# A four-block transformer kernel: scores ahead of the value fold, a bf16 bias product, an earlier opening of the last attention, and Silu on ScalarE in the last mixture

## The chip, the cores and the metric

The kernel runs on one NeuronCore of one Trainium2 chip. The metric is the device time of one execution in microseconds (us); several executions are given, and their median is the time compared. The profile is of one execution of its own.

## The reference

The input x has 4 blocks of 512 tokens of 256 numbers in float32. Four attentions and four feed-forward layers follow each other; each adds a gated term to x.

```python
x = x + tanh(g_xattn[0]) * L0_xattn(layernorm(x), ctx, mask)   # 16 heads, 64 keys, softmax per head
x = x + tanh(g_ffn[0])   * L0_ffn(layernorm(x))                # quantised gated FFN, 704 wide
x = x + tanh(g_xattn[1]) * L1_xattn(layernorm(x), ctx)         # one head
x = x + tanh(g_ffn[1])   * L1_ffn(layernorm(x))                # mixture: 8 experts, top 2, relu squared
x = x + tanh(g_xattn[2]) * L2_xattn(layernorm(x), ctx)         # one head
x = x + tanh(g_ffn[2])   * L2_ffn(layernorm(x))                # top 1, one shared weight, with bias b_expert
x = x + tanh(g_xattn[3]) * L3_xattn(layernorm(x), ctx)         # 16 heads, scores clipped to +-11
x = x + tanh(g_ffn[3])   * L3_ffn(layernorm(x))                # mixture: 8 experts, top 2, silu; shared expert
# L3_ffn: h = silu(x @ w1[e]);  y = h @ w2[e];  routed = sum of topw * y
# L2_ffn: expert_out = dispatched @ w_expert + b_expert
```

## The kernel before

The eight layers are stages 0 to 7 of one program. All five queues (SP, POOL, PE, ACT, DVE) are written out by hand, in the order of the code; an instruction waits for counts of semaphores. x stays in SBUF, and a block is four tiles of 128 tokens. Each pipe has two PSUM buffers, used in turn: `pt` for transposes, `sh` for scores and hidden values, `ob` for outputs. `product` (line 701) is nearly every matmul, `transposes` (line 669) every transposition, `move` (line 1277) ACT's copy out of `pt`.

Stage 0 begins with `fold16`. The context's keys and values are multiplied into the weights once, so that the scores of a tile are one product of 128 tokens with 1024 columns (16 heads times 64 keys), and the output one product with `valsO`. On PE that is: keys and values of the context, transposes of Wq, eight products for the folded keys (line 735), eight for the folded values (line 745). ACT moves the first half of each and DVE the second (lines 1328 to 1330 and 1746 to 1762); between them DVE has the other work of the `between` table, LayerNorm statistics and the row maxima of the quantised weights (`row_max`), after which POOL may round these weights (`to_int`, waits for `q_inv`).

`attend16(stage)` is the attention with 16 heads, in stages 0 and 6. PE does for every tile t: transposes of the probabilities of t (they wait for `prob_ready`), scores of tile t+2, output product of t. In stage 0 DVE adds the mask (L1788), takes the maximum of each head (L1791), subtracts it (L1793), waits for ACT's one Exp over 1024 columns (L1340), sums the heads (L1801), and multiplies by the reciprocals (L1805). The probabilities have two buffers. In stage 6 the scores are clipped (L1796) instead of shifted. After each block DVE takes the statistics of the new x (L1657), in stage 0 its extremes too (L1778).

Stage 5 does per block: router logits, two output products of two tiles each with the bias as a third factor (`ones[0:1]` times `be2[0:1]`, in float32), and between them the folding of stage 6's keys and values (`fold_units`, counted by `f_full` and `f_taken`).

Stage 6 opens with `fold_done`: DVE adds the bias bo3 to the folded values (L2395) after stage 5's last statistics, and PE's first scores wait for it. SP then loads w1 of the last mixture into `raw1`; POOL splits it into `wB`, four times a copy (L635) and a subtraction (L583).

The mixtures (stages 3 and 7) send the rows to DRAM by expert, fetch pairs of 128 rows back and run `NPAIR` = 20 pairs through a pipeline: transposes, product with w1 (`expert_up`), activation, transposes, product with w2 (`expert_back`). In stage 7 the activation of a pair is ACT's Tanh (L1507) and then DVE's (1 + t) * u (L2167); the missing 0.5 is in the weights wK (`weigh`).

## Time and profile before

| | us |
|---|---|
| median of 3 executions | 954.27 |
| lowest, highest | 948.47, 955.95 |
| the profiled execution, its own time | 944.84 |
| its span | 943.1 |
| PE busy in the span | 787.4 |
| DVE busy | 630.2 |
| ACT busy | 334.4 |
| POOL busy | 283.0 |

The span is the time from the first to the last instruction, 1.7 us less than the execution's own time. A busy PE is not PE at its peak. In the views a row is a start and a duration in us, the engine, the line of the program, the operation, output and inputs by their names without buffer numbers, and in brackets the idle time before it and what ended it. Stage 0's attention runs from about 63 to 214, stage 5 from about 559 to 617, stage 6 from there to about 775, and stage 7's pairs from about 832 to 910.

### The profile page before, as it was taken

What the parts mean: (1) busy time and instruction counts of PE and PEld (TensorE: products, weight loads), DVE (VectorE), ACT (ScalarE), POOL (GpSimd) and SP (SyncE); (2) the same over time, 40 slices, a digit from 0 to 9 for tenths busy, and PEclk for the clock granted to TensorE, in tenths of its full rate; (3) what the DMA queues carried; (4) which work ended last, traced back from release to release, by engine and by line L of the source; (5) the groups of instructions that cost most, each with busy time, mean ns of one, the idle gap of its engine ahead of it and who ended that gap; (6) DMA issues with size and microseconds to landing.
All of it is one profiled execution on the core that took longest, in us unless ns stands there. A gap on an engine that the chain in (4) does not pass through costs nothing.

```text
span 943.1 us, 13461 instructions
## 1 busy us (share of the span) xinstructions
PE 787.4 (83%) x4214; PEld 593.6 (63%) x4216; DVE 630.2 (67%) x1698; ACT 334.4 (35%) x622; POOL 283.0 (30%) x284
## 2 busy tenths in 40 slices
PE   7688988965788777589989799978999998779992
PEld 6455656653256656379978676635676675479971
DVE  3678889866997666555637775556757655566646
ACT  2422231225644662134544543312233221235530
POOL 1038113160001556614561111234001234205540
PEclk9998999997999999779999998889999998889995
DMA  8629950000001002247426000051000011224427
GB/s 284 123 92 385 313 187 0 1 1 1 0 1 34 1 0 86 95 122 248 137 80 223 1 1 1 1 179 34 1 1 12 35 45 47 89 58 143 134 85 255
DMA packets 55474, 83.30 MB, mean 88 GB/s; under 512 B 14688, under 2 KB 44384, under 8 KB 55136
## 3 DMA queue, kind: packets, MB, share of 16 engines
q1 hardware_dynamic: 48496, 63.52, 21.8%
q0 software_dynamic: 6912, 18.95, 5.6%
q8 instruction: 36, 0.59, 0.3%
q14 instruction: 30, 0.25, 0.1%
HBM read 61.41 MB, written 37.95 MB: 105 GB/s over the span
## 4 chain that ended last, share of the span: by engine, by line
PE 50%; DVE 24%; ACT 8%; DVEq 6%; issue 6%; DMA 3%; POOL 2%; SPq 0%; ACTq 0%; POOLq 0%
PE sh L701 12%; PE ob L701 12%; PE sh L1077 6%; PE ob L1077 6%; PE pt L669 4%; DVE sm L1801 2%; DVE x L2043 2%; DVE work L1805 2%; DVE work L1793 2%; DVE mx L1791 2%; ACT work L1340 2%; PE pt L701 2%; DVEq L1790 2%; DVE stats L1657 2%; PE pt L1069 2%
## 5 line engine op out<-in xcount | busy, mean ns | idle before, releaser
L701 PE MATMUL sh<-area,xnT 128*128 128x512 f32 (+1 forms) x384 | 138.2, 509 | 7.0 <-issue 4.5
L701 PE MATMUL ob<-area,work 128*128 128x256 f32 x512 | 116.3, 380 | 9.0 <-ACT work L1277 9.0
L534 POOL TENSOR_TENSOR rstd<-var,minush 128x4 f32<-128x4 f32 (+1 forms) x29 | 30.4, 1047 | 303.6 <-DVE var L1664 303.6
L701 PEld LDWEIGHTS ob<-area,work 128*128 128x128 f32 x512 | 96.7, 190 | 34.6 <-issue 22.8
L598 POOL DMA_INDIRECT yt<-xn,work x80 | 76.7, 959 | 122.5 <-ACT xn L1521 106.9
L701 PEld LDWEIGHTS sh<-area,xnT 128*128 128x128 f32 x384 | 64.3, 199 | 59.6 <-issue 56.4
L1340 ACT ACTIVATE work<-work 128x1024 f32<-128x1024 f32 x32 | 33.8, 1058 | 174.5 <-DVE work L1793 93.6
L589 POOL DMA_INDIRECT xg<-area,dest x64 | 63.9, 999 | 70.4 <-DVE dest L2035 53.0
L669 PE MATMUL pt<-ident,work 128*128 128x128 f32 (+1 forms) x292 | 41.9, 284 | 24.7 <-DVE work L1805 10.8
L701 PE MATMUL ob<-area 128*128 128x256 f32 (+1 forms) x152 | 45.2, 458 | 15.8 <-DVE area L2061 9.0
L669 PEld LDWEIGHTS pt<-ident,work 128*128 128x128 f32 (+1 forms) x292 | 33.8, 142 | 32.8 <-issue 14.4
L701 PEld LDWEIGHTS ob<-area 128*128 128x128 f32 (+1 forms) x152 | 32.8, 220 | 28.4 <-DVE area L2061 10.8
L1801 DVE TENSOR_REDUCE sm<-work 128x16 f32<-128x1024 f32 x32 | 38.9, 1216 | 16.3 <-ACT work L1340 16.3
L1277 ACT COPY work<-pt 128x512 f32<-128x512 f32 (+1 forms) x76 | 41.3, 582 | 16.2 <-PE pt L669 15.8
L1657 DVE BATCH_NORM_STATS2 stats<-x 128x6 f32<-128x256 f32 x128 | 45.0, 414 | 2.9
L1805 DVE TENSOR_TENSOR work<-work,rsm 128x1024 f32<-128x1024 f32 x32 | 41.0, 1282 | 2.4
L2157 DVE TENSOR_TENSOR xnTR<-pt,xnTR 128x512 fp32r<-128x512 f32 x40 | 27.6, 691 | 21.9 <-ACT xnTR L1501 21.9
L1077 PE MATMUL sh<-wB,xnTR 128*128 x240 | 35.7, 301 | 5.7 <-DVE xnTR L2157 5.7
L1507 ACT ACTIVATE work<-sh 128x512 f32<-128x512 f32 x40 | 23.9, 598 | 41.7 <-PE sh L1077 41.7
L701 PE MATMUL sh<-area 128*128 (+3 forms) x118 | 35.6, 446 | 2.9 <-DVE area L2307 2.6
L1521 ACT COPY xn<-ob 128x512 f32<-128x512 f32 x40 | 23.5, 587 | 39.8 <-PE ob L1077 29.7
L1712 DVE TENSOR_TENSOR x<-ob,x 128x256 f32<-128x256 f32 x32 | 13.4, 420 | 36.0 <-PE ob L701 36.0
(298 smaller groups left out, 1664.2 us busy)
## 6 DMA issues: line engine op xcount, KB each, us to landing
work<-xg SPq DMA_DIRECT2D x80, 129.0 KB, 2.3
area<-in_L_ffn_w SPq DMA_DIRECT2D x4, 2048.0 KB, 12.6
area<-yt SPq DMA_DIRECT2D x8, 1024.0 KB, 9.0
area<-in_L_xattn_Wq SPq DMA_DIRECT2D x2, 1024.0 KB, 9.7
x<-in_x SPq DMA_DIRECT2D x1, 2048.0 KB, 15.3
area<-in_L_xattn_Wo SPq DMA_DIRECT2D x2, 1024.0 KB, 16.0
area<-in_L_xattn_Wkv SPq DMA_DIRECT2D x2, 1024.0 KB, 6.3
out<-x SPq DMA_DIRECT2D x4, 512.0 KB, 2.9
```

The costliest lines, as they stand in the source:

```text
L534: pool.tensor_tensor(rstd[:, n], var[:, n], minush[:, n], ALU.pow).then_inc(given, 1)
L589: pool.indirect_dma_start(xg_rows[:, :], bass.IndirectOffsetOnAxis(ap=dest[:, b % 2, 2 * j + w:2 * j + w + 1], axis=0), xn_rows(stage, b)[ ...
L598: pool.indirect_dma_start(yt[:, :], bass.IndirectOffsetOnAxis(ap=back_to[:, 2 * i + q:2 * i + q + 1], axis=0), ypair[i % 2][:, q * D:(q + ...
L669: mm = pe.transpose(dst[0:r, c0:c1], src, (idn or ident)[0:src.shape[0], 0:src.shape[0]])
L701: mm = pe.matmul(o, a, b, start=(k == 0), stop=(k == len(lhs) - 1))
L1077: mm = pe.matmul(o, lhs[:, a, k * P:(k + 1) * P], w[:, b, bass.ds(off + k * D, D)], start=(k == 0 and t == 0), stop=(k == 1 and t == 2))
L1277: act.copy(dst, src[0:r, 0:cols_]).then_inc(pt_moved, 1)
L1340: act.activation(prob[i % 2], prob[i % 2], ACT.Exp).then_inc(exped[stage], 1)
L1657: dve.bn_stats(stats[:, j, :], tile(j) if tile else xt(b, j))
L1801: dve.tensor_reduce(sm[:, i % 2, :], heads(p), AX.X, ALU.add)
L1805: dve.tensor_tensor(heads(p), heads(p), over_keys(rsm[:, i % 2, :]), ALU.mult).then_inc(prob_ready[stage], 1)
L2157: dve.tensor_tensor(xnTR[:, 0, 1, (i % 2) * 512:(i % 2 + 1) * 512], pt[i % 2][:, :], xnTR[:, 0, 0, (i % 2) * 512:(i % 2 + 1) * 512].bitcas ...
```

## The change

1. Stage 0: the scores of tiles 0 and 1 stand between the folded keys and the folded values on PE. In ACT, the Exp of these tiles stands between the moves of the values; in DVE, `shift0` of both stands ahead of the values.
2. Stage 0: the maximum is no longer subtracted by DVE. It is negated and goes in as the bias of Exp, so Exp is one instruction for each head (16 of 64 columns for a tile), and each gives the head's sum by `accum_out`. DVE's mask and maximum are done in two halves of 8 heads, the first as soon as half of the scores is there (`scored_half`). The row maxima of the weights move from the fold into the first three tiles.
3. Stage 5: the bias is split into three bf16 parts in rows 0, 32 and 64 of `be2_parts` (over bo0's memory), by nine operations of DVE after a memset, ahead of the pairs of stage 3; the bias product is one of 96 rows of bf16 ones.
4. Stage 6: PE's first scores wait for `f_taken` and no longer for `fold_done`, which moves ahead of stage 5's blocks on DVE; w1 is loaded as soon as 8 units are folded, and its first part is copied by ACT (`raw_hi`) ahead of the first Exp. POOL keeps the subtractions.
5. Stage 7: the activation of a pair is ACT's Silu; DVE's instruction is gone, and the 0.5 leaves the weights.

```diff
+        SCORES0, VALUES0, FOLDED0 = start_of("sh", 0) + 12, start_of("sh", 0) + 14, start_of("sh", 0) + 22
@@ PE, fold16
+                first_norm_T(6, 1)
+                pe.wait_ge(pt_moved, 8)
+                pe.wait_ge(sh_taken, SCORES0)
+                scores16(0, 0, 0)
+                scores16(0, 0, 1)
+                n = VALUES0
@@ PE, attend16
                 if stage == 6:
+                    pe.wait_ge(sh_taken, start_of("sh", 6) + PRE["sh"][6])
+                    pe.wait_ge(f_taken, NFOLD)
+                    pe.wait_ge(pt_moved, start_of("pt", 6))
+                    scores16(6, 0, 0)
+                    scores16(6, 0, 1)
                     pe.wait_ge(fold_done, 1)
-                    pe.wait_ge(pt_moved, start_of("pt", 6))
+                else:
+                    pe.wait_ge(sh_taken, FOLDED0)
@@ PE, stage 5
-                                     [T(5, b)[:, k, j * P:(j + 1) * P] for k in range(KD)] + [ones[0:1, :]],
-                                     [wexp[:, k * D:(k + 1) * D] for k in range(KD)] + [be2[0:1, :]])
+                                     [T(5, b)[:, k, j * P:(j + 1) * P] for k in range(KD)] + [onesb[0:96, :]],
+                                     [wexp[:, k * D:(k + 1) * D] for k in range(KD)] + [be2_parts[0:96, :]])
@@ ACT
+            def exps0(i, first, last):
+                act.wait_ge(shifted[0], 2 * i + (2 if last > H // 2 else 1))
+                for h in range(first, last):
+                    p = prob[i % 2][:, h * C:(h + 1) * C]
+                    a = act.activation(p, p, ACT.Exp, bias=mx[:, i % 2, h:h + 1], accum_out=sm[:, i % 2, h:h + 1])
+                if last == H:
+                    a.then_inc(exped[0], 1)
+            def attend0():
+                for b in straight:
+                    for j in range(TB):
+                        i = b.u * TB + j
+                        for half in range(2):
+                            n = prob_fill(0, i, half)
+                            move(n, n % 2, probT[:, half * 512:(half + 1) * 512])
+                        if i + 2 < NT:
+                            exps0(i + 2, 0, H // 2)
+                        if j == 1 and b.u + 1 < NB:
+                            norm_move(0, b, 4)
+                        if i + 2 < NT:
+                            exps0(i + 2, H // 2, H)
+                act.wait_ge(in_w6, 16)
+                for b in range(NB):
+                    q = slice(b * 1024, (b + 1) * 1024)
+                    act.copy(wB[:, 0, q], raw1[:, q]).then_inc(raw_hi, 1)
+                            act.activation(hpair[m % 2], u, ACT.Silu).then_inc(h_ready[7], 1)
@@ DVE
+            def shift0(i):
+                n, slot = score_fill(0, i // TB, i % TB)
+                for c in range(2):
+                    q = slice(c * 512, (c + 1) * 512)
+                    p = prob[i % 2][:, q]
+                    dve.wait_ge(*((scored_half, i + 1) if c == 0 else (sh_full, n + 1)))
+                    ins = dve.scalar_tensor_tensor(heads(p), mask[:, i, :].unsqueeze(1).broadcast_to([P, H // 2, C]), -FMAX,
+                                                   heads(sh[slot][:, q]), ALU.mult, ALU.add)
+                    if c == 1:
+                        ins.then_inc(sh_taken, 1)
+                    dve.drain()
+                    dve.tensor_reduce(mx[:, i % 2, c * H // 2:(c + 1) * H // 2], heads(p), AX.X, ALU.max,
+                                      negate=True).then_inc(shifted[0], 1)
+            def normalise0(i):
+                p = prob[i % 2]
+                dve.wait_ge(exped[0], i + 1)
+                dve.reciprocal(rsm[:, i % 2, :], sm[:, i % 2, :])
+                dve.drain()
+                dve.tensor_tensor(heads(p), heads(p), over_keys(rsm[:, i % 2, :]), ALU.mult).then_inc(prob_ready[0], 1)
+            def attend0():
...
+                        if i >= 1:
+                            add(Block((i - 1) // TB), 0, (i - 1) % TB, [(i - 1) % TB])
+                        if i + 2 < NT:
+                            shift0(i + 2)
+                        if i + 1 < NT:
+                            normalise0(i + 1)
+                        if i < 3:
+                            row_max(i)
+                        if i == 3:
+                            weight_scales()
@@ POOL
-            pool.wait_ge(in_w7, 32)
             for b in range(NB):
                 q = slice(b * 1024, (b + 1) * 1024)
-                pool.tensor_copy(wB[:, 0, q], raw1[:, q])
-                pool.drain()
+                pool.wait_ge(raw_hi, b + 1)
                 rest(wB[:, 1, q], raw1[:, q], wB[:, 0, q], raw_split)
@@ SP
-            sp.wait_ge(f_taken, NFOLD)
+            sp.wait_ge(f_taken, 8)
+            load(raw1.rearrange("p (e n) -> p e n", e=2 * NE), rows(I["L3_ffn_w1"].rearrange("e d f -> (e d) f")), in_w6)
             sp.wait_ge(o_added, start_of("o", 6))
-            load(raw1.rearrange("p (e n) -> p e n", e=2 * NE), rows(I["L3_ffn_w1"].rearrange("e d f -> (e d) f")), in_w7)
             load(raw2.rearrange("p (e n) -> p e n", e=2 * NE), rows(I["L3_ffn_w2"].rearrange("e f d -> (e f) d")), in_w7)
```

Where the instructions stand. On PE, at the end of stage 0's fold (`area2` holds the context's values and Wo, `area1` the folded keys, `xnT` the normalised tokens, `work` the probabilities), before:

```order
L745 MATMUL sh0<-area2 128x256 [waits sh_taken]
L745 MATMUL sh0<-area2 128x256 x3
L745 MATMUL sh1<-area2 128x256 [waits sh_taken]
L745 MATMUL sh1<-area2 128x256 x3
L669 MATMUL pt0<-ident,xn 128x128 [waits pt_moved,ln_done]
L669 MATMUL pt0<-ident,xn 128x128 x3
L669 MATMUL pt1<-ident,xn 128x128 [waits pt_moved]
L669 MATMUL pt1<-ident,xn 128x128 x3
L701 MATMUL sh0<-area1,xnT 128x512 [waits sh_taken,pt_moved]
L701 MATMUL sh0<-area1,xnT 128x512 x3
L701 MATMUL sh1<-area1,xnT 128x512 [waits sh_taken]
L701 MATMUL sh1<-area1,xnT 128x512 x3
```

and now, where the last products of the folded keys (line 757) are followed by them:

```order
L757 MATMUL sh1<-work 128x256 [waits sh_taken]
L757 MATMUL sh1<-work 128x256 x3
L679 MATMUL pt0<-ident,xn 128x128 [waits pt_moved,ln_done]
L679 MATMUL pt0<-ident,xn 128x128 x3
L679 MATMUL pt1<-ident,xn 128x128 [waits pt_moved]
L679 MATMUL pt1<-ident,xn 128x128 x3
L711 MATMUL sh0<-area1,xnT 128x512 [waits sh_taken,pt_moved]
L711 MATMUL sh0<-area1,xnT 128x512 x3
L711 MATMUL sh1<-area1,xnT 128x512 [waits sh_taken]
L711 MATMUL sh1<-area1,xnT 128x512 x3
L773 MATMUL sh0<-area2 128x256 [waits sh_taken,in_wo]
L773 MATMUL sh0<-area2 128x256 x3
```

The block's first transposes and the scores of two tiles have gone ahead of the eight value products; after these the transposes of the first probabilities follow at once.

On ACT, at the start of stage 0's attention (`sm` are the heads' sums, `mx` their maxima), before:

```order
L1330 ACTIVATE area1<-sh1,gates 128x512 [waits sh_full]
L1277 COPY xnT<-pt0 128x512 [waits pt_full]
L1277 COPY xnT<-pt1 128x512 [waits pt_full]
L1340 ACTIVATE work<-work 128x1024 [waits shifted0] x2
L1277 COPY work<-pt0 128x512 [waits pt_full]
L1277 COPY work<-pt1 128x512 [waits pt_full]
```

and now, from the last value move on:

```order
L1362 ACTIVATE area1<-sh1,gates 128x512 [waits sh_full]
L1298 COPY work<-pt0 128x512 [waits pt_full]
L1298 COPY work<-pt1 128x512 [waits pt_full]
L1321 ACTIVATE work,sm<-work,mx 128x64 [waits shifted0]
L1321 ACTIVATE work,sm<-work,mx 128x64 x7
L1321 ACTIVATE work,sm<-work,mx 128x64 [waits shifted0]
L1321 ACTIVATE work,sm<-work,mx 128x64 x7
```

One Exp of 1024 columns for a tile has become two groups of eight, and it now stands behind the moves of the tile two before it.

On PE, where stage 6 opens, before (`prob_ready6` is that tile 0's probabilities are there):

```order
L701 MATMUL ob1<-be2,ones 128x256
L701 MATMUL sh0<-area1,xnT 128x512 [waits pt_moved,sh_taken,fold_done]
L701 MATMUL sh0<-area1,xnT 128x512 x3
L701 MATMUL sh1<-area1,xnT 128x512 [waits sh_taken]
L701 MATMUL sh1<-area1,xnT 128x512 x3
L669 MATMUL pt1<-ident,work 128x128 [waits pt_moved,prob_ready6]
```

and now:

```order
L711 MATMUL ob1<-bo0,onesb 128x256
L711 MATMUL sh0<-area1,xnT 128x512 [waits pt_moved,sh_taken,f_taken]
L711 MATMUL sh0<-area1,xnT 128x512 x3
L711 MATMUL sh1<-area1,xnT 128x512 [waits sh_taken]
L711 MATMUL sh1<-area1,xnT 128x512 x3
L679 MATMUL pt1<-ident,work 128x128 [waits pt_moved,prob_ready6,fold_done]
```

The wait for `fold_done` has moved behind both scores.

## Rows read from the trace of the kernel before

**Rows 1.** TensorE in order of time, stage 0's attention.
```profile
74.28 1.97 PE L669 MATMUL pt<-ident,work 128*128 128x128 f32 x8 [4.46 <-DVE work L1805]
76.04 5.71 PE L701 MATMUL sh<-area,xnT 128*128 128x512 f32 x8
...
137.35 1.04 PE L669 MATMUL pt<-ident,work 128*128 128x128 f32 x8
138.22 3.60 PE L701 MATMUL sh<-area,xnT 128*128 128x512 f32 x8
...
145.11 1.04 PE L669 MATMUL pt<-ident,work 128*128 128x128 f32 x8
...
204.60 3.69 PE L701 MATMUL ob<-area,work 128*128 128x256 f32 x16 [3.14 <-ACT work L1277]
...
209.99 3.69 PE L701 MATMUL ob<-area,work 128*128 128x256 f32 x16 [0.82 <-ACT work L1277]
```

**Rows 2.** Busy time of each engine in one stretch of it.
```profile
73.90:200.40 126.50, 116.32 (x472) 79.14 (x473) 111.59 (x148) 31.45 (x48) 46.57 (x36) 0.97 0.47 156
```

**Rows 3.** VectorE in order of time, stage 0's attention.
```profile
97.72 1.23 DVE L1805 TENSOR_TENSOR work<-work,rsm 128x1024 f32<-128x1024 f32 x1
...
105.80 1.23 DVE L1805 TENSOR_TENSOR work<-work,rsm 128x1024 f32<-128x1024 f32 x1
...
113.28 2.34 DVE L1778 TENSOR_REDUCE xmm<-x 128x4 f32<-128x1024 f32 x2
```

**Rows 4.** ScalarE in order of time: a tile's two moves, and stage 2's Exp.
```profile
103.68 1.05 ACT L1277 COPY work<-pt 128x512 f32<-128x512 f32 x2
...
305.72 0.35 ACT L1417 ACTIVATE work<-work,mx 128x64 f32<-128x64 f32 x1 [1.81 <-DVE mx L1870]
306.07 0.33 ACT L1417 ACTIVATE work<-work,mx 128x64 f32<-128x64 f32 x1
```

**Rows 5.** All engines in order of time, stage 0's folded values.
```profile
56.12 2.00 PE L745 MATMUL sh<-area 128*128 128x256 f32 x8 [0.38 <-DVE area L1762]
57.51 0.74 DVE L1762 TENSOR_SCALAR area<-sh,gates 128x512 f32<-128x512 f32 x1
```

**Rows 6.** TensorE in order of time, one pair of products of stage 5.
```profile
585.15 0.69 PE L701 MATMUL ob<-be,ones 1*128 1x256 f32 x2
585.77 1.13 PE L701 MATMUL ob<-area,xnT 128*128 128x256 f32 x4
```

**Rows 7.** The chain that ended last, in order of time.
```profile
278.66 3.35 PE ob L1217 x24
...
616.88 4.46 issue
621.34 6.20 PE sh L701 x8
...
653.46 5.13 PE sh L701 x8
```

**Rows 8.** VectorE and TensorE in order of time, stages 5 and 6.
```profile
573.86 1.38 DVE L1670 TENSOR_SCALAR xn<-x,mv,rstd 128x256 f32<-128x256 f32 x4
...
619.97 1.27 DVE L2395 SCALAR_TENSOR_TENSOR area<-bo,gates,area 64x1024 f32<-64x1024 f32 x1
...
632.81 1.09 PE L669 MATMUL pt<-ident,work 128*128 128x128 f32 x8 [1.85 <-DVE work L1805]
...
642.79 2.21 DVE L1805 TENSOR_TENSOR work<-work,rsm 128x1024 f32<-128x1024 f32 x1
644.92 4.26 DVE L1670 TENSOR_SCALAR xn<-x,mv,rstd 128x256 f32<-128x256 f32 x4
```

**Rows 9.** GpSimd in order of time, the last subtraction of the split.
```profile
646.04 2.35 POOL L583 TENSOR_TENSOR wB<-area,wB 128x1024 fp32r<-128x1024 f32 x1
```

**Rows 10.** VectorE and TensorE: start of stage 3's and of stage 7's pairs.
```profile
405.67 0.69 DVE L2157 TENSOR_TENSOR xnTR<-pt,xnTR 128x512 fp32r<-128x512 f32 x1 [8.72 <-ACT xnTR L1501]
...
841.89 1.67 PE L1077 MATMUL ob<-wA,hidR 128*128 x12 [0.58 <-DVE hidR L2182]
```

More of the change, by code:

```diff
@@ L702, in product, with scores16 @@
                 return mm
+            def scores16(stage, u, j):
+                n, slot = score_fill(stage, u, j)
+                sh_slot(n)
+                for c in range(2):
+                    mm = product(sh[slot][:, c * 512:(c + 1) * 512],
+                                 [T(stage, Block(u))[:, k, j * P:(j + 1) * P] for k in range(KD)],
+                                 [keysA[:, (k * NB + u) * H * C + c * 512:(k * NB + u) * H * C + (c + 1) * 512]
+                                  for k in range(KD)])
+                    if stage == 0 and c == 0:
+                        mm.then_inc(scored_half, 1)
+                mm.then_inc(sh_full, 1)
             def fold16(stage, cT_, in_k, in_v, in_q, in_o, loads):
@@ L794, in attend16 @@
                         if j < 2:
-                            scores(b.u, j + 2)
+                            scores16(stage, b.u, j + 2)
                         elif b.u + 1 < NB:
@@ new lines, in normalise0 @@
+            def normalise0(i):
[5 more added lines that the diff above has]
+            def attend0():
+                for b in straight:
+                    for j in range(TB):
+                        i = b.u * TB + j
+                        pb = Block(b.u - 1)
+                        if i >= 1:
[8 more added lines that the diff above has]
+                            weight_scales()
+                        if b.u >= 1 and j == 0:
+                            norm_stats(pb)
+                        if b.u >= 1 and j == 1:
+                            extremes(pb)
+                        if i == 0:
+                            norm_next(0, straight[0], xn_free(0, straight[0], 5))
+                        if j == 3 and b.u + 2 < NB:
+                            norm_next(0, straight[b.u + 1], xn_free(0, straight[b.u + 1], 5))
+                add(straight[-1], 0, TB - 1, [TB - 1])
+                norm_stats(straight[-1])
+                extremes(straight[-1])
@@ L2035, in place, with bias_parts @@
                 dve.tensor_copy(dest[:, b.u % 2, :], destf[:, :, :].rearrange("p j w -> p (j w)")).then_inc(placed[stage], 1)
+            def bias_parts():
+                dve.memset(be2_parts[:, :], 0.0)
+                for r, before in ((0, 0), (32, 1), (64, 2)):
+                    row, part = be2[r:r + 1, :], be2_parts[r:r + 1, :]
+                    for _ in range(before):
+                        dve.drain()
+                        dve.tensor_copy(part, row)
+                        dve.drain()
+                        dve.tensor_tensor(row, row, part, ALU.subtract)
+                    dve.drain()
+                    ins = dve.tensor_copy(part, row)
+                ins.then_inc(bias_split, 1)
             def combine(stage, b):
@@ L2389, in route5 @@
                     ins.then_inc(o_added, 1)
+            v0 = valsO[0:64, 0:NB * D].rearrange("p (b d) -> p b d", b=NB)
+            dve.wait_ge(f_taken, 14)
+            dve.scalar_tensor_tensor(v0, bo3[0:64, :].unsqueeze(1).broadcast_to([64, NB, D]), gates[0:64, 3:4], v0,
+                                     ALU.mult, ALU.add).then_inc(fold_done, 1)
             for b in straight:
```

154 lines of the change are left out of this document (63 added, 91 removed).

## The prediction, made before the changed kernel ran

> **What bounds the kernel now.** I read the chain of waits first, by engine and then in order of time, and after it the timelines of the stages that the diff touches. PE carries half of the chain; DVE's part lies in stage 0 and at the openings. So each edit is worth what PE waits there, or what it takes away from PE's own stream.
>
> Stage 0's attention: in the middle of a block the transposes of successive tiles stand 7.76 us apart with no idle before them (137.35 to 145.11), the transposes taking 0.87 and the rest being scores and outputs [rows 1]. PE is the bound there, and DVE just keeps up: 8.1 us from one tile's normalising to the next (97.72 to 105.80 [rows 3]), for five passes over 1024 columns of about 1.23 and an Exp between them. Where DVE also has a block's extremes (2.34) and statistics, PE starves. From 73.90 to 200.40 PE is busy 116.32 of 126.50, so it stands idle for 10.2 [rows 2]. At the start it waits 4.46 for the first probabilities, and its first scores then take 5.71 instead of 3.60, since its clock has fallen to the lower level after that idle time [rows 1]. At the end it waits 3.14 for ACT, whose Exp and moves follow DVE [rows 1].
>
> Stage 5 is PE's own stream. The opening of stage 6 is a wait: PE ends stage 5 at 616.88, then nothing for 4.46 (`fold_done`, which DVE reaches at 619.97 behind the last statistics) [rows 7, 8], then two scores at the lower clock, the first 6.20 [rows 7], then 1.85 more until tile 0's probabilities at 632.81 [rows 8]. At tile 2 it waits again: a normalisation on DVE takes 2.21 and the four of xn 4.26, where the same four take 1.38 in stage 5, and the scores after that stall again run slowly, 5.13 [rows 7, 8].
>
> **The change part by part.** Sums are against the profiled execution's 944.84 us, of which 943.1 is the span.
>
> *Stage 0, loop.* For a tile DVE now has two half masks and two half maxima of 512 columns, each about 0.69 (such an operation of 512 columns takes 0.69 [rows 10]), and normalising 1.23 plus a small reciprocal [rows 3], with the add about 5 us against 7.76. ACT has 16 Exps at a pitch of 0.35 (305.72 to 306.07, with the accumulator's read inside it, the nearest row there is) and two moves of 1.05: 5.6 + 1.1 = 6.7 [rows 4]. Both fit under PE. So do the waits, counted from the end of a tile's scores, S. The first half was there 1.7 earlier, so its Exps run from S - 0.2 to S + 2.6, the second half's to S + 5.4, and the next moves to S + 6.5; the output product that needs them starts at S + 7.76. DVE ends the second half at S + 1.4 and the normalising of the next tile at S + 3.0; PE's transposes want it at S + 3.45. The margin is 0.45, the thinnest of the plan. A block's statistics or extremes (2.1 and 2.34) now lie in the time in which DVE waits for the next half score.
>
> PE's own work is then: 14 tiles of 7.76, 108.6; the last two without scores, 5.4 each (204.60 to 209.99 [rows 1]), 10.8; three transposes of a new block with their moves, about 1.4 each, 4.2. Together 123.6. Before, from 74.28 to 209.99 + 3.69 = 213.68, it was 139.4. Gain 15.8 at most. I take 14.5, leaving 1.3 for the first three tiles, where DVE has the row maxima (about 1.9 each) besides.
>
> *Stage 0, opening.* PE leaves the folded keys at about 41. The first block's transposes and their moves bring it to 43.4, two scores of 3.5 to 50.5. Eight value products of 2.00 [rows 5] would end at 66.5 if nothing waited. DVE holds them up: the first value's three operations (2.8), normalising tile 0 (1.6), and the statistics of two blocks (2.1 each) come between; by hand I get 69.2 for the last product and, with a move on ACT and DVE's 0.74 [rows 5], 70.6 for the start of the loop, against 74.28. ACT's Exps of both tiles (5.6 each) lie beside it. Gain 3.7. The bounds are 0 (the fold stretches by as much as it overlaps) and 5.
>
> *Stage 5.* The float32 bias takes 0.62 (585.15 to 585.77 [rows 6]), 16 times. A bf16 product of 128 by 256 takes 3.35 / 24 = 0.14 in stage 1 [rows 7]. 16 x 0.48 = 7.7; if changing from 128 rows to 96 and back costs as much again, 16 x 0.34 = 5.4. I take 7.5, since nothing else is late there: DVE idles for 6 us in a block. The split costs DVE a memset and nine operations of one row, 2 to 4 us, in a wait of 8.72 before stage 3's first pair [rows 10]: nothing; without that cover it would cost all of it. The earlier addition of bo3 (1.27 [rows 8]) delays stage 5's first block on DVE, whose one-hots are there some 2 us before PE asks.
>
> *Stage 6, opening.* Let E be the end of stage 5. The scores follow at once, at the full clock, to E + 6.9 (3.44 each, the pace of 138.22 in [rows 1]). DVE needs E + 3.4 for the last block's statistics, then clips at E + 3.6, and Exp, sum, reciprocal and product make E + 8.8 for PE's first transposes. Before it was 632.81 - 616.88 = 15.9. Gain 7.1. ACT's four copies (about 1 each) begin when its last small move is done, 3 before E, and end at E + 1, ahead of the first Exp at E + 4.9. They cost nothing unless w1 is late; it is loaded a hundred us earlier, behind the loads of stage 3's results. POOL's subtractions start behind its own last rstd, at E + 7.9, and take 4 x 2.35 [rows 9] to E + 17.4. The xn of the next block comes at E + 19.8, so it should take 1.38 and not 4.26, and the stall and slow scores after it go: 4.3 more by the same count of steps (its scores end 21.5 after the first transposes instead of 653.46 + 5.13 - 632.81 = 25.8 [rows 7, 8]). Gain 11.4.
>
> Those rows show DVE's operations between SBUF and SBUF stretched while POOL works, 4.26 for 1.38. The Trainium skill (GPSIMD Engine Reference, Key points) says that GpSimd shares its SBUF interfaces with VectorE and contends with instructions in a 2-port mode or with two SBUF inputs. By that rule the subtractions, which stay, still meet the normalising of tiles 0 and 1. The rival on this below is priced from rows.
>
> *Stage 7.* The pairs are PE's stream without gaps, so DVE's 0.69 less per pair is worth nothing there. Only at the start DVE's instruction stands ahead of one that PE waits 0.58 for [rows 10]. Gain 0.6; one more table load on ACT falls in a wait of 8 us for the first product. From -1.3 to 1.
>
> Sum: 14.5 + 3.7 + 7.5 + 11.4 + 0.6 = 37.7. That is 944.84 - 37.7 = 907 for an execution like the profiled one. The median before is 954.27, 9.4 above the profiled one, and the three range over 7.5. I put the same distance on the new kernel: 954.27 - 37.7 = 916.6. I say **916**.
>
> **The rivals.**
>
> *ACT becomes the bound in stage 0.* If the accumulator's read doesn't hide behind the next head's Exp and a head costs half as much again as in [rows 4], 0.54, a tile costs 16 x 0.54 + 1.05 = 9.7, and the loop's 14 tiles take 27 us more than PE's work: the loop loses about 12 on before instead of gaining 14.5. 37.7 - 26.5 = 11: **943**. Against it stands the pitch in [rows 4]. 6%.
>
> *The margin of 0.45 isn't there.* DVE's second half, drains and semaphores take a microsecond more than by my count, or POOL's rounding of the weights, which now runs beside the loop's tiles 4 to 14, stretches the normalising. Then PE waits about 0.6 a tile: 14 x 0.6 = 8.4, and **925**. For it: in [rows 8] such a product took 2.21. Against it: in tiles with POOL at work in stage 0 it took 1.23 [rows 3]. 17%.
>
> *The collision in stage 6 stays.* The subtractions run into the xn of the second block as before, because they start later or are themselves slowed: the 4.3 are lost, and 1 or 2 of the 7.1 with the normalising of tiles 0 and 1. **922**. This is where that rule of the Trainium skill leads. 15%.
>
> *The fold only stretches.* The scores' 7 us are added to the fold, since DVE and ACT paced it before, and the opening gives 0: **920**. 12%.
>
> *Slower.* The per-head Exps again, at a dearer price. The loop took 9.04 a tile before (126.50 / 14 [rows 2]); the rest of the change gives 23.2, or 1.66 a tile. So the whole is slower once ACT takes 10.7 a tile, that is 0.60 a head. At 0.65 (a wait for each accumulator before the next head) a tile is 11.5 and the total about 12 us slower than before, **966**. The row's 0.35 speaks against it; that the bias and sum here are columns of a 16-wide tile instead of 4 changes nothing that I can see. 2%.
>
> *It doesn't do what it says.* DVE's passes leave, but stage 0 isn't shorter, since PE's 7.76 bound it already. Only the idle 10.2, the slow start and the end can be won, and if all of these come from something else (the blocks' new xn, say), stage 0 gives 3: **932**. 3%.
>
> **How the numbers follow.** The forecast, 916, has 45%. With the next four rivals (925, 922, 920 and 932) lying within 16 us of it, 92% lies between about 905 and 935; the runs' own spread of some 4 us either way is in that. The range is **903 to 934**: at the low end all bounds on the good side (16 + 5 + 9 + 12 + 1 = 43) and a run like the profiled one. Faster by over 1% (below 944.7, which is about what a measurement of this kernel can tell from no change) is 94%: the forecast and all rivals but the two of ACT, and most of the first of these. Within 1%: 4%. Slower by over 1%: 2%.
>
> **What the profile after would show.** Right: the first attention's transposes 7.8 apart across block boundaries too, PE idle there under 3 us, the first probabilities' transposes at 70 to 71; the bias product at 0.14 to 0.2; PE without a gap from stage 5 into the scores, tile 0's transposes 9 us after it; xn of the next block at 1.4; pairs still 3.7 apart. Wrong: waits of PE for DVE's L1847 in every tile, or for ACT's moves (ACT late), an Exp pitch over 0.4, or POOL's subtractions beside an xn over 3 us. What would upset the sum most is a median whose distance from the profile isn't that of before.

## The result, and the profile after

| | before | after |
|---|---|---|
| median, us (4 executions each) | 953.74 | 914.34 |
| lowest, highest | 948.47, 955.95 | 911.95, 922.32 |
| span of the profiled execution | 943.1 | 910.2 |

The ratio is 0.9609, with a 95% interval from 0.9538 to 0.9681; 916 was forecast.

I cut both traces at the same instructions of PE, and set the differences beside the terms of the sum (us; the stretch from stage 1 to the start of stage 5 has no term):

| stretch | before | after | gain | forecast |
|---|---|---|---|---|
| to the first probabilities' transposes | 74.28 | 73.05 | 1.2 | 3.7 |
| stage 0's loop | 139.2 | 124.8 | 14.4 | 14.5 |
| stages 1 to 4 | 345.3 | 349.6 | -4.4 | 0 |
| stage 5 | 58.1 | 42.5 | 15.6 | 7.5 |
| stage 6 to its second router product | 115.4 | 108.2 | 7.1 | 11.4 |
| from there to stage 7's first product with w2 | 109.7 | 107.6 | 2.1 | 0.6 |
| the pairs from there on | 68.3 | 71.5 | -3.2 | 0 |
| the rest | 33.0 | 33.0 | 0 | 0 |

The total is near the forecast, but three of its terms are not. The experiments are about those.

Stage 0's loop in the trace after, TensorE in order of time (start, duration; it answers to [rows 1]):

```profile
73.05 1.07 PE L679 MATMUL pt<-ident,work 128*128 128x128 f32 x8 [1.68 <-issue]
...
137.97 1.04 PE L679 MATMUL pt<-ident,work 128*128 128x128 f32 x8
138.84 3.60 PE L711 MATMUL sh<-area,xnT 128*128 128x512 f32 x8
...
145.73 1.04 PE L679 MATMUL pt<-ident,work 128*128 128x128 f32 x8
...
188.96 3.69 PE L711 MATMUL ob<-area,work 128*128 128x256 f32 x16 [1.82 <-ACT work L1298]
```

and its loop as one stretch (columns as in [rows 2]):

```profile
73.05:197.87 124.82, 121.19 (x521) 85.62 (x522) 88.05 (x161) 94.39 (x486) 58.00 (x45) 1.00 0.56 185
```

The pitch is 7.76 still, but now in every tile, over block boundaries too: PE idles 3.6 in the whole loop, where it idled 10.2 in [rows 2], and the clock is 1.00 instead of 0.97. DVE's busy time fell and ACT's rose, and neither is waited for. How near DVE is to being waited for, its own rows show:

```profile
128.66 1.38 DVE L1847 TENSOR_TENSOR work<-work,rsm 128x1024 f32<-128x1024 f32 x1
...
136.42 1.23 DVE L1847 TENSOR_TENSOR work<-work,rsm 128x1024 f32<-128x1024 f32 x1
```

The second ends at 137.65, and PE's transposes that need it start at 137.97: a margin of 0.32, and 0.17 in the tile before, whose normalising took 1.38. The forecast had 0.45.

The start of stage 6, TensorE:

```profile
589.73 0.27 PE L711 MATMUL ob<-bo,onesb 96*128 96x256 bf16 x1
589.85 7.03 PE L711 MATMUL sh<-area,xnT 128*128 128x512 f32 x16
601.06 1.92 PE L679 MATMUL pt<-ident,work 128*128 128x128 f32 x8 [4.19 <-issue]
602.78 4.46 PE L711 MATMUL sh<-area,xnT 128*128 128x512 f32 x8
```

and what VectorE and GpSimd do meanwhile:

```profile
597.98 2.99 DVE L1891 TENSOR_TENSOR work<-work,rsm 128x1024 f32<-128x1024 f32 x1
...
604.84 1.74 DVE L1891 TENSOR_TENSOR work<-work,rsm 128x1024 f32<-128x1024 f32 x1
...
613.83 1.38 DVE L1715 TENSOR_SCALAR xn<-x,mv,rstd 128x256 f32<-128x256 f32 x4
```

```profile
597.54 11.25 POOL L595 TENSOR_TENSOR wB<-area,wB 128x1024 fp32r<-128x1024 f32 x4
```

E is the end of stage 5, 590.0 here. Scores follow it without a gap, as forecast, and the next xn takes 1.38, where it took 4.26 in [rows 8]. But GpSimd's subtractions begin 0.44 ahead of tile 0's normalising, which takes 2.99 instead of 1.23, and that operation is the one PE waits for: E + 11.1 instead of E + 8.8. After the wait of 4.19 the granted clock is at the lower of its two levels for a while, and the next score takes 4.46 for 3.60.

### The profile page after: what moved, and what is told of

Its sections match the earlier page's. It is cut to its first block, busy times and chain, and to the rows that moved or that the text cites. A ratio compares the mean times of both kernels' runs of the same rounds, so it can differ in the third digit from the quotient of the medians.

```text
span 910.2 us, 13905 instructions
## 1 busy us (share of the span) xinstructions
PE 763.5 (84%) x4198; PEld 583.2 (64%) x4200; DVE 584.1 (64%) x1688; ACT 408.5 (45%) x1123; POOL 276.2 (30%) x280
## 4 chain that ended last, share of the span: by engine, by line
PE 59%; DVE 16%; ACT 8%; issue 7%; DVEq 4%; another core or an unknown queue 2%; DMA 2%; POOL 1%; SPq 0%; ACTq 0%; POOLq 0%
PE sh L711 18%; PE ob L711 16%; PE pt L679 6%; PE ob L1098 5%; PE sh L1098 4%; DVE x L2135 2%; PE pt L711 2%; DVE stats L1702 2%; PE pt L1090 2%; PE ob L1237 1%; ACT work L1321 1%; DMA work<-xg 1%; PE sh L1117 1%; PE sh L773 1%
## 5 line engine op out<-in xcount | busy, mean ns | idle before, releaser
L711 PE MATMUL sh<-area,xnT 128*128 128x512 f32 (+1 forms) x384 | 133.2, 494 | 1.6 <-ACT area L1656 1.0
L711 PEld LDWEIGHTS sh<-area,xnT 128*128 128x128 f32 x384 | 62.3, 194 | 51.2 <-issue 48.5
L1321 ACT ACTIVATE work<-work,mx 128x64 f32<-128x64 f32 x256 | 85.1, 334 | 21.6 <-DVE mx L1839 21.6
L711 PE MATMUL ob<-area 128*128 128x256 f32 (+1 forms) x152 | 40.4, 420 | 17.2 <-DVE area L2153 7.1
L1298 ACT COPY work<-pt 128x512 f32<-128x512 f32 (+1 forms) x76 | 41.3, 581 | 18.8 <-PE pt L679 18.0
L2251 DVE TENSOR_TENSOR xnTR<-pt,xnTR 128x512 fp32r<-128x512 f32 x40 | 27.6, 690 | 34.3 <-ACT xnTR L1545 30.6
L1321 ACT ACTIVATION_READ_ACCUMULATOR work<-work,mx 128x1 f32 x256 | 48.0, 187 | 0.0
L711 PEld LDWEIGHTS ob<-area 128*128 128x128 f32 (+1 forms) x152 | 29.4, 198 | 28.4 <-issue 9.5
L1384 ACT ACTIVATE work<-work 128x1024 f32<-128x1024 f32 x16 | 16.9, 1059 | 66.4 <-DVE work L1882 66.4
L1567 ACT COPY xn<-ob 128x512 f32<-128x512 f32 x40 | 23.6, 590 | 43.5 <-PE ob L1098 34.4
L1834 DVE SCALAR_TENSOR_TENSOR work<-mask,sh 128x512 f32<-128x512 uint8 x32 | 22.0, 687 | 26.9 <-PE sh L711 26.9
L2272 DVE TENSOR_TENSOR hidR<-sh,hidR 128x512 fp32r<-128x512 f32 x40 | 27.5, 686 | 17.1 <-ACT hidR L1561 15.4
## 6 DMA issues: line engine op xcount, KB each, us to landing
area<-in_L_xattn_Wq SPq DMA_DIRECT2D x2, 1024.0 KB, 10.2
```

The source lines that it names most:

```text
L711: mm = pe.matmul(o, a, b, start=(k == 0), stop=(k == len(lhs) - 1))
L1298: act.copy(dst, src[0:r, 0:cols_]).then_inc(pt_moved, 1)
L1321: a = act.activation(p, p, ACT.Exp, bias=mx[:, i % 2, h:h + 1], accum_out=sm[:, i % 2, h:h + 1])
L1567: act.copy(ypair[m % 2], ob[m % 2][:, :]).then_inc(y_moved[stage], 1)
L2251: dve.tensor_tensor(xnTR[:, 0, 1, (i % 2) * 512:(i % 2 + 1) * 512], pt[i % 2][:, :], xnTR[:, 0, 0, (i % 2) * 512:(i % 2 + 1) * 512].bitcas ...
L2272: dve.tensor_tensor(hidR[:, 0, 1, (m % 2) * 512:(m % 2 + 1) * 512], sh[1][:, (m % 2) * 512:(m % 2 + 1) * 512], hidR[:, 0, 0, (m % 2) * 512 ...
```

## The experiments

**The changed kernel once more.**

> The changed kernel once more, for a second profile. In the first one VectorE and ScalarE have idle times that no semaphore explains (ScalarE 2.5 to 3.5 us before four of the last Silus, VectorE 0.5 to 1 us in stage 3's routing), which the trace of before hardly has; together they cost TensorE about 7 us. If they belong to the program (its instructions lie otherwise, so that an engine runs out of them at the same places), they stand at the same places again, and the execution takes 912 again. If they are chance, they are elsewhere or gone, and an execution without them takes about 905.

Ratio 0.9621 [0.9566, 0.9677], span 908.8. The idle times are not at the same instructions, but in the same stretches: in stage 3's routing, in its pairs, and from the middle of stage 7's pairs, which took 72.7. Neither branch of the expectation fits whole. From stage 1 to the start of stage 5 it took 349.5. In the three kernels below whose stages 1 to 4 are those of before, apart from the split of the bias in one, it took 351.0 (b_bias), 352.2 (b_rows) and 356.1 (b_silu). So the 345.3 in the trace of before is the exception, and most of the loss of 4.4 in my table is no effect of the change. One part is: the split of the bias. In the trace after, at the start of stage 3's pairs, ScalarE, VectorE and TensorE:

```profile
392.38 0.59 ACT L1545 CAST xnTR<-pt 128x512 fp32r<-128x512 f32 x1 [12.13 <-PE pt L1090]
393.64 0.28 DVE L2126 CAST bo<-be 1x256 bf16<-1x256 f32 x1
393.96 0.69 DVE L2251 TENSOR_TENSOR xnTR<-pt,xnTR 128x512 fp32r<-128x512 f32 x1
394.90 2.92 PE L1098 MATMUL sh<-wA,xnTR 128*128 x12 [1.61 <-DVE xnTR L2251]
```

VectorE is still at the split when ScalarE's cast is done (392.97), and TensorE's first product waits for the operation behind it. That operation starts 0.99 after the cast, where it starts 0.03 after it in all three traces without the split. In the eleven with it, it is 0.03 twice and 0.36 to 3.06 in the others, with a median of 1.2.

**Stage 5: the bf16 bias alone, on the kernel before.** The edit is part 3 of the diff and nothing else.

> The kernel before with the bf16 bias product alone. Stage 5 lasts 58.1 us in the trace of before (558.76 to 616.88) and 42.5 in that of after; the prediction had 7.5 of these 15.6. Theory A: the float32 products of one row also lower the granted clock (0.80 in two of the four blocks before, 1.00 after), so the whole 15.6 comes back with this edit alone: stage 5 at 42 to 43, clock 1.00, the kernel at 0.985 of before. Theory B: the clock there is lower because of the stages ahead, which this edit doesn't change: stage 5 at 50 to 51, clock 0.80 in two blocks, the kernel at 0.992.

**A float32 bias with all rows, on the kernel before.**

```diff
-  ... + [ones[0:1, :]],   ... + [be2[0:1, :]])
+  ... + [ident[:, :]],    ... + [be2[:, :]])
```

> The kernel before with a bias product of all 128 rows, still float32: the identity matrix times be2, whose 128 rows are all the bias; the same result and, by its columns, the same duration of 0.62. Theory A (products of one row don't count as work for the clock): the clock is 1.00 in all four blocks, and stage 5 takes 58.1 - 6 = 52 us. Theory B (not the rows but something else, the time that these products take or the stages ahead): clock 0.80 in two blocks and 58 us as before.

b_bias: ratio 0.9859 [0.9794, 0.9924], stage 5 at 42.1. b_rows: ratio 0.989 [0.9821, 0.9959], stage 5 at 47.2. The products of b_rows, TensorE:

```profile
581.06 0.59 PE L701 MATMUL ob<-be,ident 128*128 128x256 f32 x2
581.49 1.03 PE L701 MATMUL ob<-area,xnT 128*128 128x256 f32 x4
582.35 0.59 PE L701 MATMUL ob<-be,ident 128*128 128x256 f32 x2
```

and of the kernel before, the row that follows [rows 6]:

```profile
586.84 0.69 PE L701 MATMUL ob<-be,ones 1*128 1x256 f32 x2
```

From one bias product to the next it is 1.29, against 1.69 with one row (in the trace of before, 585.15 in [rows 6] to the row below) and 0.98 with the bf16 rows (572.18 to 573.16 after). So I had mis-sized the product: same columns, same type, but one row of weights costs 0.40 more here than 128, part of it in the product behind it (1.07 to the next start, against 0.86 in b_rows and after). TensorE's weight loads show where it goes, in before and in b_rows:

```profile
585.15 0.29 PEld L701 LDWEIGHTS ob<-be,ones 1*128 1x128 f32 x2 [0.33 <-issue]
585.77 0.73 PEld L701 LDWEIGHTS ob<-area,xnT 128*128 128x128 f32 x4 [0.33 <-issue]
```

```profile
580.84 0.41 PEld L701 LDWEIGHTS ob<-be,ident 128*128 128x128 f32 x2
581.27 0.84 PEld L701 LDWEIGHTS ob<-area,xnT 128*128 128x128 f32 x4
```

With one row, the loads pause for 0.33 before it and again behind it; with 128 rows, and with the 96 bf16 rows after, they don't. From a pair's first product to what follows its second bias product it is 3.35 with one row (at the upper clock), 2.77 in b_rows and 2.12 after; eight pairs times 1.23 is 9.8. Now the clock, in one block of stage 5 each (the columns as in [rows 2], the granted clock third from the end): before, after, b_rows, and b_silu, a kernel of a later experiment that has before's stage 5 unchanged (its stretch is counted from the fold's products, and 0.1 short of a block).

```profile
571.70:588.50 16.80, 16.08 (x82) 10.68 (x80) 8.32 (x44) 4.81 (x11) 3.15 (x6) 0.80 0.00 0
```

```profile
558.25:569.43 11.18, 10.35 (x79) 8.11 (x77) 8.23 (x45) 4.72 (x11) 2.03 (x5) 1.00 0.00 1
```

```profile
578.30:590.76 12.46, 11.63 (x82) 9.40 (x81) 8.24 (x44) 4.72 (x11) 3.16 (x6) 1.00 0.00 1
```

```profile
582.50:596.00 13.50, 12.67 (x80) 8.78 (x80) 8.32 (x44) 4.72 (x11) 3.16 (x6) 1.00 0.00 1
```

Theory A of both expectations would have stopped at the first three. The fourth takes its general form away: with the same one-row products the clock was 1.00 all through, and stage 5 took 52.1. So in the stage's 15.6, 9.6 is the products at an equal clock (52.1 to 42.5; 4.9 of it from one row to 128, 4.7 from there to the 96 bf16 rows), and 6.0 is a lower clock that one of two executions with one-row products had. Whether such products make that fall likelier stays open: no trace without them shows it in stage 5, but two with them are too few. In that block of before PE was busy for 16.08 of 16.80 and idle for 0.72 at a time at most. The 42.1 of b_bias against 42.5 says that the rest of the change costs 0.4 here: after, PE waits 0.85 in the first block for ScalarE's moves of the transposed xn, and in b_bias 0.47.

**Stage 0: the scores behind the values again.** On the changed kernel; SCORES0 goes, the five lines on PE move behind the loop over the values, and ACT's and DVE's with them.

> The changed kernel with the scores of tiles 0 and 1 behind the folded values again (on TensorE, ScalarE and VectorE); the rest of part 2 stays, the Exp of each head too. The first probabilities' transposes stand at 73.05, 71.02 and 70.83 in three traces with early scores, at 74.28, 76.74 and 75.19 in three traces without the change. Theory A (the prediction's: the scores hide the longer Exp of these two tiles, 16 Exps at 0.35 instead of one of 1.06): the first transposes come at 76 to 78, the kernel is 5 us slower than after. Rival B (the fold stretches by what it overlaps, and the gain came from the row maxima that left the fold): 71 to 73, no difference from after. The loop takes 124.8 from there by both.

Ratio 0.9631 [0.9552, 0.971]. The first transposes stand at 73.68, by neither theory. The start of every execution varies, so I count from the last product of the folded keys: before's order with before's Exp 34.3, 35.8, 35.0 and 34.9 (four traces); the eight traces with early scores and halves 29.8 to 32.4, but once 35.0, where the scores ran partly at the lower clock (9.69 for 7.13), with a median of 31.1; this kernel 32.8. So by the medians 2.1 of a gain of 3.9 is there without early scores, as rival B has it, and the early scores bring 1.8. That is from one trace without them, and traces of one order differ by 1.5 and more, so the shares are rough. The Exps of 16 heads did not delay tile 0; that its first half begins while the second half is being scored is an argument for it, and the next kernel, with early scores and no halves, stands at 34.4. The size of the term was right (3.9 for 3.7), its reason only in part.

**Stage 0: the mask and the maximum in one piece.** On the changed kernel:

```diff
-                for c in range(2): ...   # halves of 512 columns, the first on scored_half
+                dve.wait_ge(sh_full, n + 1)
+                dve.scalar_tensor_tensor(heads(p), <mask>, -FMAX, heads(sh[slot][:, :]), ALU.mult, ALU.add)...
+                dve.tensor_reduce(mx[:, i % 2, :], heads(p), AX.X, ALU.max, negate=True).then_inc(shifted[0], 2)
```

> The changed kernel with the mask and the maximum of a tile in one piece of 1024 columns, begun when the whole score is there. The pitch is 7.76 a tile with halves. Theory A (ScalarE's order sets the margin): the mask and maximum end 2.5 after a tile's scores, 16 Exps of 0.35 end 8.1 after them, and the next tile's moves, which stand behind them on ScalarE, come about 1.4 too late for the output product that TensorE begins 7.76 after the scores: some 1.4 a tile, 20 in all, the kernel at 935 and the loop at 145 instead of 124.8. Rival B (the halves are not needed, since a tile's probabilities are wanted only two tiles later): loop 125 to 128.

Ratio 0.9848 [0.977, 0.9926], 937.4. The loop takes 141.8. TensorE:

```profile
143.26 3.69 PE L711 MATMUL ob<-area,work 128*128 128x256 f32 x16 [0.49 <-ACT work L1298]
...
151.88 3.69 PE L711 MATMUL ob<-area,work 128*128 128x256 f32 x16 [0.50 <-ACT work L1298]
```

Output products wait for ACT's moves and the pitch is 8.62: theory A, with 0.9 a tile for 1.4. Without the halves the loop is slower than before's 139.2. Trading DVE's passes for 16 Exps on ScalarE, in this order of its work, would have gained nothing by itself; the half-score handed over early is what turns it into time.

**Stage 6: the subtractions later.** On the changed kernel, one line ahead of POOL's loop:

```diff
+            pool.wait_ge(prob_ready[6], 2)
```

> The changed kernel with GpSimd's four subtractions of stage 6 held back until tile 1's probabilities are normalised. In the traces of after the normalising of tile 0 takes 2.99 and that of tile 1 1.74, beside the subtractions, where others take 1.23; TensorE's first transposes of probabilities come 11.06 after the end of stage 5. Theory A (the collision on VectorE's path is the cause): 1.23 each, the transposes 9.3 after the end of stage 5, the wait before them 2.4 instead of 4.2, and the kernel 1.8 to 2.7 faster than after. Rival B (what is late is not this: the statistics, the clip and the Exp ahead of it): 11 as before. The subtractions then run beside tiles 2 and 3, where VectorE waits for TensorE 2 us a tile, which should hide it.

Ratio 0.9637 [0.9543, 0.9731], no gain on after. Tile 0's normalising takes 1.23 and the first transposes come 9.31 after E, all as in theory A. Then VectorE and TensorE:

```profile
611.25 3.20 DVE L1892 TENSOR_TENSOR work<-work,rsm 128x1024 f32<-128x1024 f32 x1
```

```profile
620.82 1.94 PE L680 MATMUL pt<-ident,work 128*128 128x128 f32 x8 [1.89 <-ACT xnT L1411]
```

The last subtractions meet tile 2's normalising and the next xn (3.40 for 1.38), and PE waits there instead: 21.24 from the first transposes to the scores of tile 4, where it was 19.86. The wait had only moved.

**Stage 6: the subtractions in two pairs, where VectorE has no such work.** On the changed kernel:

```diff
             for b in range(NB):
+                pool.wait_ge(prob_ready[6], 2 if b < 2 else 4)
```

> The changed kernel with GpSimd's four subtractions of stage 6 in two pairs, begun when tile 1's and when tile 3's probabilities are normalised. With all four behind tile 1 the first transposes came 9.3 instead of 11.06 after the end of stage 5, but the third and fourth subtraction met tile 2's normalising (3.20 instead of 1.23) and the next xn, and from these transposes to the fourth following scores it was 21.24 instead of 19.86. Two take about 4.7, and VectorE's next operation between SBUF and SBUF starts 6.4 after the first signal and 8 after the second. Theory A (a place exists where they cost nothing): 9.3 and 19.9, 1.8 us less than after. Rival B (they cost the same wherever they stand): the sum stays at 30.5 to 30.9.

Ratio 0.9593 [0.9556, 0.9629]. VectorE:

```profile
599.89 1.23 DVE L1892 TENSOR_TENSOR work<-work,rsm 128x1024 f32<-128x1024 f32 x1
...
611.16 1.23 DVE L1892 TENSOR_TENSOR work<-work,rsm 128x1024 f32<-128x1024 f32 x1
612.30 1.38 DVE L1716 TENSOR_SCALAR xn<-x,mv,rstd 128x256 f32<-128x256 f32 x4
```

No normalising or xn is stretched; first transposes at E + 9.3, and 27.5 from E to the scores of tile 4 instead of 30.9: 1.8 from the collision, and 1.7 because the clock stayed at the upper level behind a wait of 2.42. It did so behind the 2.43 of d_rest too, but in the run best below the same wait of 2.43 was followed by 0.91 of the clock up to the scores of tile 4, and by 29.2. The timed executions don't tell 2 or 3 us from nothing. The rule of the Trainium skill (GPSIMD Engine Reference, Key points), that GpSimd and VectorE contend for their shared SBUF interfaces when VectorE's instruction has two SBUF inputs, agrees: normalising reads two tiles of SBUF and took 1.23 alone and 1.74 to 3.20 beside the subtractions. The four operations of xn read one tile of SBUF and were stretched as well (4.26 in [rows 8] and 3.40 in d_rest, for 1.38); whether they fall under its other case, an instruction in a 2-port mode, no view here shows.

**Stage 7: the gate as before, on the changed kernel; and Silu alone, on the kernel before.** Part 5 of the diff, undone in the one, done in the other.

> The changed kernel with stage 7's gate as before (ScalarE's Tanh, VectorE's (1 + t) * u, the 0.5 in the weights). From the first product with w2 to the end of the pairs it is 68.3 us in the trace of before (841.89 to 910.15) and 71.5 in that of after. Theory A (Silu takes work from VectorE, costs ScalarE nothing and has nothing to do with the four idle times): those stay, the pairs take 71 to 72. Theory B (the idle times belong to Silu or to the way it stands among the waits): without it the pairs take 68.3 and the kernel is 3 us faster than after. By either the first product with w2 comes 0.6 to 1.1 later.

> The kernel before with Silu in stage 7 alone. The pairs, from the first product with w2 to their end, took 68.2 in all four traces with Tanh (68.26, 68.20, 68.19, 68.18) and 71.5 and 72.7 in the two with Silu, which have idle times of ScalarE ahead of Silu that no semaphore explains. Theory A (they come with Silu): 71 to 73 here too, and the kernel 2 to 3 us slower than before. Rival B (chance, or something else in the changed kernel): 68.2, and by the 0.6 to 1.1 that the first product with w2 comes earlier the kernel is as fast as before.

u_silu: ratio 0.963 [0.957, 0.969], the median equal to that of the run beside it (913.57 and 913.8), its pairs 68.20. b_silu: ratio 1.0062 [1.0021, 1.0102], 0.6% slower than before by an interval that only just leaves 1 out, its pairs 73.2. Of all traces with Silu, each has 71.5 to 73.8 for the pairs; those with Tanh and VectorE's instruction have 68.2 to 68.3 four times, and 69.5 once (best). The time is lost as here in after, ScalarE and then TensorE:

```profile
853.77 0.60 ACT L1555 ACTIVATE work<-sh 128x512 f32<-128x512 f32 x1 [3.52 <-remote]
```

```profile
855.70 1.70 PE L1098 MATMUL ob<-wA,hidR 128*128 x12 [0.52 <-DVE hidR L2272]
```

ScalarE idles 2.5 to 3.5 before every second Silu and PE's next product is about 0.8 late, here from the middle of the pairs on and in other traces from the first quarter on. "remote" says that the view finds no instruction for the signal that ended the wait. The product that this Silu reads is recorded to end at 851.00, 2.8 us before; in before, Tanh starts 0.04 after it (864.11 and 864.15). The semaphore records in the trace tell more. The count of the products with w1, which this Silu waits for, is raised at 853.74, just before the Silu and 2.7 after the product's recorded end. Three more of TensorE's counts, for groups recorded to end at 851.44, 852.86 and 853.31, follow by 853.99. So ScalarE does wait, and for TensorE, whose signals come late and together. In every trace, each wait of ScalarE over 2 us marked "remote" ends like this, with a count of TensorE raised 1.5 to 3.7 after the recorded end. Whether TensorE was late or only its signals, and why, the traces don't say, since the ends of its products are modelled.

Part 5 was forecast at a gain of 0.6. At the first product u_silu has 108.1, and the traces with Silu on the changed kernel have 107.1 to 109.5, so no gain can be told from their spread. In the pairs it loses 3.3 to 5.6.

**The function or the order.** Both on the changed kernel:

```diff
 s_tanh:
-   act.activation(hpair[m % 2], u, ACT.Silu).then_inc(h_ready[7], 1)
+   act.activation(hpair[m % 2], u, ACT.Tanh, scale=0.5).then_inc(h_ready[7], 1)
 s_dve:
+   act.activation(hpair[m % 2], u, ACT.Silu).then_inc(relu_ready, 1)      # ACT
+   dve.tensor_copy(h[:, 0:1], h[:, 0:1]).then_inc(h_ready[7], 1)           # DVE
```

> The changed kernel with ScalarE's Tanh in the place of its Silu and still no instruction of VectorE behind it (left out: the factor (1 + t) * u; the pairs compute something else, with the same sizes). In the pairs ScalarE idles 3.1 to 3.4 us before every second activation, from about the middle on, in all six traces with Silu, and in none of four with Tanh and VectorE's instruction. Theory A (the idle times come from the order of work, ScalarE handing over to TensorE with nothing between): the pairs take 71 to 73 here too. Theory B (the function Silu itself): 68.2.

> The changed kernel with Silu, and behind it an instruction of VectorE that copies one column of the result onto itself (128 numbers) and then tells TensorE, as the old gate did. Theory A (the order of work): the step over VectorE brings back the old rhythm, the pairs take 68.2. Theory B (the function): 71 to 73.

One execution each: 919.92 and 915.28. The pairs take 73.8 in both, with the idle times in both. So Silu is not needed for them: Tanh has them too when nothing stands between ScalarE and TensorE. But an instruction of VectorE in between doesn't end them either, if it is short; so theory A is right about the function and wrong about the hop. What differs from the quiet kernels is that the hidden value is handed over some 0.5 to 0.7 us earlier (VectorE's instruction of 0.69 is missing). That and repeated idle times go together in all traces; best has a single one without it. Silu with an instruction of VectorE as long as the old one, which would test this, was not run, and the mechanism stays open.

**Both mends.** The changed kernel with before's gate and the subtractions in two pairs.

> The changed kernel with both mends: the subtractions in two pairs as in the run beside it, and stage 7's gate as before, with Tanh and VectorE. From the traces: 1.8 us less at the opening of stage 6, the pairs at 68.2 instead of 71.5 to 73.1, their first product with w2 0.7 later: 4.3 to 6 us less than after in all, a span of 903 to 906, a ratio to before of 0.955 to 0.958. If Silu's loss were something that only the profiled executions show, the time would equal that of the run beside it.

Ratio 0.9528 [0.949, 0.9566], 910.87: the fastest of all, 5.5 below the run beside it with Silu (916.4, 0.9593 [0.9556, 0.9629]), whose interval it just touches. It is a little below the 0.955 to 0.958 forecast, which the interval still reaches. The pairs took 69.5 and had one idle time. Its trace had a span of 909.4, not the 903 to 906 forecast: from stage 1 to stage 5 it took 355.2, against 349.6 in after, with nothing changed there.

## Why the prediction was right, and where it was right by luck

- **Stage 0's loop.** Right by its own steps: bounded by PE at 7.76, ACT at 6.7 a tile, a margin forecast at 0.45 and found at 0.17 to 0.32. Nine traces with the changed loop give 124.8 to 125.0, four with the old one 139.2 to 139.3, so the gain is 14.4; forecast 14.5. Without the halves a tile takes 0.86 more, near the 0.6 of the rival of the missing margin, but PE waits mostly for ACT's moves and not for DVE.
- **Stage 0's opening.** Its size was right (3.9 for 3.7). I had all of it from the overlap with the fold; about half is there without it.
- **Stage 5.** The mechanism was right and the term mis-sized: "16 x 0.48 = 7.7". It took the product alone, from its start to the next, and not the pause in the weight loads behind it; at an equal clock the stage gains 9.6. The profiled executions differ by 6.0 more by the clock, which no view of before could promise and which isn't in every execution.
- **The split of the bias on VectorE, taken at nothing.** It took 4.15, a little over the "2 to 4 us", and "a wait of 8.72" did not cover it: VectorE reached it 24.7 after the last router product, where in before it was free 18.8 after it, and in nine of eleven traces the first pair had to wait. That cost 1.0 in the trace after and 0 to 3.0 in all. From the last router product of stage 3 to the first product with w2 it is 37.1, 38.2 and 40.5 in the kernels without the split and 36.9 to 39.7 in those with it, so the stretch as a whole varies by more than this.
- **Stage 6's opening.** The step that failed is "POOL's subtractions start ... at E + 7.9", with nothing charged for it. They started at E + 7.5, 0.4 ahead of the normalising that PE waits for, and took 11.25 instead of 4 x 2.35. Of the 7.1, 4.9 came: 1.8 is this collision, and 0.5 the count of steps, since the transposes come at E + 9.3 and not E + 8.8 even without it (d_rest, d_spread, best). The xn collision went as forecast; but of its 4.3 only 2.3 came, since the longer wait let the clock fall once more. This was the rival "the collision in stage 6 stays" by half: not with xn, but with tile 0.
- **Stage 7.** "The pairs are PE's stream without gaps, so DVE's 0.69 less per pair is worth nothing there" left out that the new order might bring gaps. It lost 3.3 to 5.6 us, outside the bounds of -1.3 to 1.
- **The chances.** "Faster by over 1%" at 94% leaves out most of the 6% for 943, which lies below 944.7; by its own terms it is 95% or more.
- **The sum.** Against its term stage 5 brought 2.1 more (8.1 in the profiled pair), stage 6 4.3 less and stage 7 1.7 less. The distance from profile to median, taken as 9.4 for the new kernel, was 2.4 there: the profiled execution of before was a quick one in stages 1 to 4 (345.3, where the others with its code there have 352 and 356). A median 39.4 lower for a forecast of 37.7 is good fortune in part; the two terms that carry most of it, stage 0 and stage 5, were understood.

## What to carry to other kernels

Taking passes off an engine that just keeps pace gains only if the chain from one tile to the next gets shorter too: here a hand-over at half a score, worth 17 us of the loop. A piece of background work that shares an engine's memory paths has a right place in the tile; look for the gap in which the victim has none of the operations seen to stretch (here the normalising and xn), and count how long it is before choosing how many pieces go there. Compare several traces of the same code with each other before calling a difference of a few us an effect.

## What I had not expected of the hardware

A float32 product of one row by 256 columns costs more than one of 128 rows by 256 columns: 1.69 against 1.29 with the four products beside it, and the weight loads pause for 0.33 before it and behind it. TensorE's granted clock averaged 0.80 over each of two blocks of stage 5, though in that stage PE had not been idle for more than 0.72 at a time before it; in another execution of the same code it stayed at 1.00. After a wait of 2.4 it fell in one execution and not in two others. TensorE's signals come 1.5 to 3.7 after the recorded end of the work now and then, several within 0.25, and ScalarE waits for them; this is in all traces here but the one of before. In the kernels whose last activation hands its result over 0.5 to 0.7 us earlier, such waits come again and again and the 20 pairs take 3.3 to 5.6 longer.
